# Warm-up matmuls in groups behind landings, last blocks loaded in parts, last deviation by a matmul, and step 1's output added by GpSimd

## What is computed

```python
def _gn(v, G=32, eps=1e-05):
    g = v.reshape(B_, G, C_ // G, H_, W_)
    m = jnp.mean(g, axis=(2, 3, 4), keepdims=True)
    s = jnp.var(g, axis=(2, 3, 4), keepdims=True)
    return ((g - m) / jnp.sqrt(s + eps)).reshape(v.shape)
def step(prev, x_i):
    y = jnp.einsum('oc,nch->noh', Wc, prev) + conv_b[None, :, None]
    y = jnp.where(y >= 0, y, prelu_a * y)
    cur = y + x_i
    return (cur, cur)
x = jnp.moveaxis(feature, 3, 0)
_, fwd_rest = jax.lax.scan(step, x[0], x[1:])
fl = jnp.concatenate([x[0:1], fwd_rest], axis=0)
_, bwd_rest = jax.lax.scan(step, fl[-1], fl[:-1], reverse=True)
out = jnp.concatenate([bwd_rest, fl[-1:]], axis=0)
...
x = x + _L0_conv_ref(_gn(x), L0_conv_conv_w, L0_conv_conv_b, L0_conv_prelu_a)
```

## Time and the profile before

| | us |
|---|---|
| median of 3 runs | 387.96 (387.77 to 388.16) |
| the profiled execution | 387.43 |
| its span | 385.7 |
| TensorE busy in it | 349.6 |
| VectorE busy in it | 288.8 |
| ScalarE busy in it | 225.6 |

### The profile page before, as it was taken

The page is one execution under the profiler, slowest core; times in us unless marked ns, Lnnn a source line. Parts: engine busy times, 40 slices in busy tenths (PEclk is TensorE's granted clock), DMA queues, the critical chain, the costliest instruction groups (busy, mean ns, idle before and its releaser), DMA issues.

```text
span 385.7 us, 10022 instructions
## 1 busy us (share of the span) xinstructions
PE 349.6 (91%) x3062; PEld 348.4 (90%) x3062; DVE 288.8 (75%) x945; ACT 225.6 (59%) x802; POOL 17.7 (5%) x24
## 2 busy tenths in 40 slices
PE   0116899999999999999999999999999999999993
PEld 0116899999999999999999999999999999999993
DVE  2886688888888878765565787787778778778774
ACT  3654265665665565566566566556656656655653
POOL 1177100000000000000000000000000000000000
PEclk9999899999999999999999999999999999999998
DMA  8997000000000000000000022112212212211222
GB/s 289 425 418 284 0 2 1 0 0 0 1 0 0 1 0 0 1 0 0 0 0 0 27 81 82 69 67 83 81 55 82 82 54 82 82 66 70 82 79 85
DMA packets 11242, 26.31 MB, mean 68 GB/s; under 512 B 1377, under 2 KB 2273, under 8 KB 11233
## 3 DMA queue, kind: packets, MB, share of 16 engines
q1 hardware_dynamic: 11088, 26.22, 17.7%
q10 hardware_dynamic: 144, 0.00, 0.0%
HBM read 13.63 MB, written 12.58 MB: 68 GB/s over the span
## 4 chain that ended last, share of the span: by engine, by line
PE 89%; DMA 6%; SPq 3%; DVE 1%; issue 1%; ACT 0%; DVEq 0%
PE psum L236 86%; DMA xin<-in_x 6%; SPq L171 3%; PE psum L218 1%; PE psum L208 1%; ACT above L273 0%; DVE state L373 0%; PE psum L197 0%; DVEq L47 0%; DVE state L368 0%; PE psum L190 0%; DVE bstat L285 0%; DVE chan L299 0%; ACT below L275 0%; PE psum L192 0%
## 5 line engine op out<-in xcount | busy, mean ns | idle before, releaser
L236 PE MATMUL psum<-state,w_t 128*128 (+1 forms) x2976 | 332.8, 275 | 0.2 <-DVE state L373 0.2
L236 PEld LDWEIGHTS psum<-state,w_t 128*128 128x128 f32 x2976 | 332.5, 192 | 0.5 <-DVE state L373 0.3
L273 ACT ACTIVATE above<-psum,params 128x128 f32<-128x128 f32 x376 | 139.7, 372 | 139.3 <-PE psum L236 129.0
L368 DVE TENSOR_TENSOR state<-above,state 128x128 f32 (+1 forms) x376 | 108.3, 288 | 70.0 <-ACT above L273 62.5
L275 ACT ACTIVATE below<-psum,negative 128x128 f32<-128x128 f32 x376 | 140.0, 372 | 0.0
L373 DVE SCALAR_TENSOR_TENSOR state<-below,negative,state 128x128 f32 (+1 forms) x376 | 123.4, 349 | 7.0 <-DVE state L368 0.4
L408 DVE TENSOR_TENSOR state<-state,xin (+1 forms) x48 | 32.9, 684 | 0.0
L285 DVE BATCH_NORM_STATS2 bstat<-xin 128x6 f32<-128x512 f32 (+2 forms) x38 | 23.1, 649 | 10.0 <-DMA xin<-in_x 9.9
L320 DVE TENSOR_SCALAR state<-xin,mean,rstd 128x320 f32<-128x320 f32 (+2 forms) x69 | 27.2, 437 | 0.2 <-POOL rstd L434 0.2
L190 PE MATMUL psum<-chan,same_group 128*128 128x4 f32 (+2 forms) x10 | 2.4, 310 | 27.1 <-DVE chan L299 27.1
L190 PEld LDWEIGHTS psum<-chan,same_group 128*128 128x128 f32 x10 | 2.1, 262 | 27.4 <-issue 15.1
(11 more groups left out here) (20 smaller groups left out, 19.9 us busy)
## 6 DMA issues: line engine op xcount, KB each, us to landing
out_y<-state SPq DMA_DIRECT2D x47, 256.0 KB, 2.0
xin<-in_x SPq DMA_DIRECT2D x14, 768.0 KB, 14.8
xin<-in_x SPq DMA_DIRECT2D x5, 256.0 KB, 3.5
w_t<-in_w SPq DMA_DIRECT2D x4, 256.0 KB, 11.6
out_y<-state SPq DMA_DIRECT2D x4, 64.0 KB, 1.7
xin<-in_x SPq DMA_DIRECT2D x1, 128.0 KB, 16.9
xin<-in_x SPq DMA_DIRECT2D x2, 64.0 KB, 14.8
params<-in_par ACTq DMA_DIRECT2D x1, 2.5 KB, 3.0
```

The costliest lines, as they stand in the source:

```text
L236: mm = nc.tensor.matmul(psum[:, 4 * par + o, 0:COLS], w_t[:, k, o * P:(o + 1) * P], xs[k], start=k == 0, stop=k == 3)
L273: nc.scalar.activation(above[:, par, o, :], z, ACT.Relu, bias=params[:, o:o + 1], scale=1.0).then_inc(above_done, 1)
L368: nc.vector.tensor_tensor(sts[o], above[:, par, o, :], sts[o], ALU.add).then_inc(part_done, 1)
```

## The change

The twelve warm-up matmuls go. In their place stand six groups (`keep_up`), each behind a landing and each a loop with two matmuls in a turn: 8 matmuls behind block 10, 6 behind block 12, 4 behind the second part of block 13, 4 and 6 behind the two parts of block 14, and 4 behind the second part of block 15. Block 0 is loaded in one piece, and blocks 13 and 14 in two (16 and 32 columns). ScalarE reduces the first unit of blocks 13 and 15 and none of block 14. The deviations and variances of a batch are read by VectorE after the first and second unit of the next tile's first block. For the last batch, of one column, a matmul with `centre` (one on the diagonal less `same_group`) gives the deviation, and one VectorE operation squares it. Step 0's matmuls stand in another order, two of them ahead of the last batch. GpSimd's early products follow each its difference. Column 1 is added by GpSimd into `spare`, the place of column 47, once that column is stored. The tiles of column 0 are stored as three and one.

```diff
-FIRST_A = [(0, 0), (0, 1), (0, 2), (0, 3)]
-FIRST_B = [(1, 0), (1, 1), (1, 2), (1, 3), (2, 0), (2, 1), (3, 0), (3, 1), (2, 2), (3, 2), (2, 3), (3, 3)]
+FIRST = [[(0, 0), (0, 1)],
+         [(1, 0), (2, 0), (0, 2), (0, 3), (1, 1), (1, 2)],
+         [(3, 0), (2, 1), (3, 1), (2, 2), (3, 2), (1, 3), (2, 3), (3, 3)]]
...
-FIRST_PIECES = [16, 16, 16]
-LAST_PIECES = [16, 16, 8, 4, 4]
+PIECES = {13: [16, 32], 14: [16, 32], 15: [16, 16, 8, 4, 4]}
+
+BY_ACT = {**{b: 2 for b in (0, 1, 2, 4, 5, 6, 8, 9, 10, 12)}, 13: 0, 15: 0}
...
+KEEP_UP = {(10, 0): 4, (12, 0): 3, (13, 1): 2, (14, 0): 2, (14, 1): 3, (15, 1): 2}
...
-            for i in range(FWD):
+            for i in range(FWD - 1):
                 step = W - 1 - i
                 sp.wait_ge(out_ready, i + 1)
-                sp.dma_start(out[step], state[:, step, :, :]).then_inc(stored, 16)
-            for o in range(KT):
-                sp.wait_ge(state_ready, 4 * (STEPS - 1) + o + 1)
-                sp.dma_start(out[0, :, o, :], state[:, 0, o, :]).then_inc(stored, 16)
-            sp.wait_ge(stored, 16 * (FWD + KT))
+                sp.dma_start(out[step], state[:, step, :, :]).then_inc(early_stored if i == 0 else stored, 16)
+            sp.wait_ge(spare_ready, 1)
+            sp.dma_start(out[1], spare).then_inc(stored, 16)
+            sp.wait_ge(state_ready, 4 * (STEPS - 1) + KT - 1)
+            sp.dma_start(out[0, :, 0:KT - 1, :], state[:, 0, 0:KT - 1, :]).then_inc(stored, 16)
+            sp.wait_ge(state_ready, 4 * STEPS)
+            sp.dma_start(out[0, :, KT - 1, :], state[:, 0, KT - 1, :]).then_inc(stored, 16)
...
+                if n1 - n0 == 1:
+                    nc.tensor.matmul(gdev, centre[:, :], chan[:, k, n0:n1, 0], start=True, stop=True).then_inc(dev_done, 1)
...
+            def keep_up(b, i):
+                pe.wait_ge(x_loaded[b][i], 16)
+                with pe.Fori(0, KEEP_UP[b, i]):
+                    for _ in range(2):
+                        nc.tensor.matmul(idle, same_group[:, :], same_group[:, :], start=True, stop=True)
...
+                if n1 - n0 == 1:
+                    dve.wait_ge(dev_done, 1)
+                    nc.vector.tensor_scalar(dev2[:, k, n0:n1], gdev, gdev, None, ALU.mult).then_inc(dev2_done, 1)
+                    dve.wait_ge(gmean_done, t + 1)
...
-            loop(dve, FWD, STEPS, slot_out)
+            loop(dve, FWD, STEPS - 1, slot_out)
+            slot(False)(STEPS - 1, (STEPS - 1) % 2)
...
+            pool.wait_ge(early_stored, 16)
+            pool.wait_ge(state_ready, 4 * (STEPS - 1))
+            nc.gpsimd.tensor_tensor(spare.rearrange("p k (n h) -> p (k n) h", n=N), state_step(pool, 1),
+                                    xin_step(pool, 1), ALU.add).then_inc(spare_ready, 1)
```

More of the change, by code:

```diff
@@ L145, in units @@
         def units(b):
[L147 to L153, removed]
+            found = []
+            begin = 0
+            for i, size in enumerate(pieces(b)):
+                for w0 in range(begin, begin + size, UNIT):
+                    found.append((w0, min(w0 + UNIT, begin + size), i))
+                begin += size
+            return [(w0, w1, i, BY_ACT.get(b) == nth) for nth, (w0, w1, i) in enumerate(found)]
         def record(b, i):
@@ L162, in scan_program @@
         act_blocks = [b for b in range(NBLK) if any(u[3] for u in units(b))]
+        spare = state[:, W - 1, :, :]
         block = ctx.enter_context(nc.Block())
@@ L213, in _ @@
             pe.wait_ge(group_made, 1)
-            for t in range(len(BATCHES) - 1):
-                if t == len(BATCHES) - 2:
-                    pe.wait_ge(x_loaded[NBLK - 2][0], 16)
-                    for _ in range(WARM_UP):
-                        nc.tensor.matmul(psum[:, 5, 0:P], same_group[:, :], same_group[:, :], start=True, stop=True)
+            pe.wait_ge(centre_made, 1)
+            for t in range(2):
                 group_means(t)
                 group_variances(t)
-            last = len(BATCHES) - 1
-            group_means(last)
-            first_units(FIRST_A)
-            group_variances(last)
-            first_units(FIRST_B)
+            keep_up(10, 0)
+            group_means(2)
+            group_variances(2)
+            keep_up(12, 0)
+            keep_up(13, 1)
+            keep_up(14, 0)
+            keep_up(14, 1)
+            keep_up(15, 1)
+            group_means(3)
+            group_variances(3)
+            first_units(FIRST[0])
+            group_means(4)
+            group_variances(4)
+            first_units(FIRST[1])
+            first_units(FIRST[2])
             def slot(forward):
@@ L286, in unit_stats, with block_stats @@
                                           x_part(b, w0, w1))
-            def block_stats(b):
-                for i, (_, _, _, by_act) in enumerate(units(b)):
-                    if not by_act:
+            def block_stats(b, between=()):
+                between = list(between)
+                for i, u in enumerate(units(b)):
+                    if not u[3]:
                         last = unit_stats(b, i)
+                        if between:
+                            between.pop(0)()
                 last.then_inc(stats_done, 1)
@@ L315, in variances @@
                 dve.wait_ge(gvar_done, t + 1)
[L316 to L317 removed]
+                nc.vector.tensor_scalar(var_eps[:, k, n0:n1], gvar(t), EPS, None, ALU.add).then_inc(var_done, 1)
             def normalise(n, k, w0, w1):
@@ L328, in _ @@
             for b in range(NBLK - 1):
-                block_stats(b)
+                t = b // N - 1
+                block_stats(b, (lambda: deviations(t), lambda: variances(t)) if t >= 0 and b % N == 0 else ())
                 if b % N != 0:
@@ L351, in _ @@
             dve.wait_ge(rstd_done, 4)
-            normalise(0, 3, 0, EARLY)
-            variances(4)
-            normalise(1, 3, 0, EARLY)
-            normalise(2, 3, 0, EARLY)
+            for n in range(N - 1):
+                normalise(n, KT - 1, 0, EARLY)
+                if n == 0:
+                    variances(4)
             dve.wait_ge(mean_kept, 5)
@@ L430, in _ @@
                                     channel_multiplier=-1).then_inc(group_made, 1)
+            pool.wait_ge(group_made, 1)
+            nc.gpsimd.tensor_scalar(centre[:, :], same_group[:, :], -1.0, None, ALU.mult).then_inc(centre_step, 1)
+            pool.wait_ge(centre_step, 1)
+            nc.gpsimd.affine_select(out=centre[:, :], in_=centre[:, :], compare_op=ALU.not_equal,
+                                    fill=1.0 - 1.0 / GROUP, base=0, pattern=[[-1, P]],
+                                    channel_multiplier=1).then_inc(centre_made, 1)
             pool.wait_ge(counts_set, 2)
```

64 lines of the change are left out of this document (33 added, 31 removed).

## The result

The changed kernel took 381.87 us (median of 4 runs, 380.97 to 382.78), the kernel before 387.87 beside it: a ratio of 0.9849, 95% interval 0.9813 to 0.9885. So the change is worth 4.8 to 6.0 us; 4.45 was forecast, and both medians lie in the range given. Two things are not as in the prediction: the terms that make up the sum, and how far apart the runs of this one kernel lie, 379.68 to 383.11 in ten.

The account below looks back on a forecast made before the run. TensorE's recurrence was taken to bound the kernel, leaving only time before step 1 and after the last step: 387.43 - 2.4 - 0 - 2.05 = 383.0, plus 0.53 for the runs' median, 383.5 us; range 381.3 to 385.3.

Parts of the forecast that it names:

- three things that were to show it wrong: Clock falling before step 1, groups ending well before or after 38.7, or step 1's store still under way at the last tile.
- The end, 2.4: After the last step: GpSimd adds column 1 early, so the last store issues at 381.15 instead of 383.51; gain 2.4 us.
- 0.5 us of cover: At the end: if GpSimd slows VectorE's addition for step 2, that has 0.5 us to spare before the next tile.
- The loads, 0 (at most 0.2): Loads of x: same bytes in 22 loads, and VectorE's long idle time ended on TensorE; 0, at most 0.2 us either way.
- The groups, 0 (from +1.8 to -0.3): Warm-up groups before step 0: end at 38.7 as before, gain 0; +1.8 for an end at 36.9, -0.3 at 39.0.
- full clock through the groups: Rival, warm-up: matmuls behind block 10 keep TensorE at full clock, groups end at 36.9; 6.25 us less, 381.7; chance 0.22.
- The order after the last statistic: Last statistic to step 1: step 1 at +4.3 instead of +6.35 us, gaining 2.05; with low clock about +5.7, gaining 0.6.
- The rule that I weighed against the row: Trainium skill's rule: clock falls come from long idle gaps between matmul bursts; by it no fall would come before step 1.
- the sparse stretch: From 38.7 to 40.7, before the first step: TensorE busy 0.74 of 2.00 us, after which the granted clock fell.

Follow-up runs that it names:

- the run with thirds: The changed kernel with block 0 loaded in three parts again instead of whole: 383.99 us, ratio 0.9915.
- The second trace: Profiled execution, 383.11 us, of the changed kernel run again with no edit; that series has a median of 382.77 us.

## Why the prediction was right

The number was right, and most of the working behind it was not. Two of the three things that were to show it wrong came about: the clock fell before step 1 in both traces of the changed kernel, and the groups ended at 35.16 and 37.29, well before 38.7. The forecast of 383.5 rested on 2.4 + 0 + 2.05. Point by point:

- **The end, 2.4: right in its mechanism, 0.2 to 0.5 too large.** It was 2.2 in the trace and 1.9 alone. GpSimd took 1.58 us where the nearest row had 1.04, which was hidden, and it slowed VectorE beside it, which was not quite: 0.2 on the path. I had given it 0.5 us of cover for the addition of step 2; the operation it met was the next one.
- **The loads, 0 (at most 0.2): wrong.** This is the first of two steps that failed. I argued that the same number of loads and bytes, and an idle time that ends on TensorE, leave nothing. But the warm-up matmuls were themselves behind block 14's landing, so a landing moved the idle time's end, and the whole load of block 0 moved every landing. Alone it gave 1.6 us. I knew of that wait and did not price an earlier landing. In the changed kernel the last landing came 1.1 to 1.2 us earlier than before; block 0's load accounts for 0.2 to 0.4 of that by the run with thirds, and where the rest comes from is not shown.
- **The groups, 0 (from +1.8 to -0.3): right for the common execution, and missed as a distribution.** The forecast's 38.7 was a start at 31.5 and 7.2 us of work. The second trace has 7.29 us of work from 30.00 on, the first 5.60 from 29.55 on. The earlier starts come with the earlier landings. Whether the rise comes in the groups or ahead of them decides their length, and it does not come at a fixed place. I had "full clock through the groups" as a rival with 0.22, for all executions; it is a case of single executions.
- **The order after the last statistic: the two values, 4.3 at the full clock and 5.7 with a fall, came out as 4.48 and 5.83.** The single instants fit too: behind the last statistic the squared deviation was done at 0.69 us (0.7 forecast) and GpSimd's power at 2.08 (2.1). But I took the full clock for the likelier, and that is the second step that failed. In both traces of the changed kernel the clock fell. The 2.05 was 0.5 there. The rule that I weighed against the row, that only long idle gaps bring a fall, does not tell this case: the clock fell at 37.80 with TensorE busy for 2.96 of the 3.40 us ahead of it. Nor does the sparse stretch bring the fall each time: where the rise came late, at 35.77 without the matmuls behind block 10 and at 38.70 with the old warm-up, the clock held through the same stretch.

So the sum of the common execution, read from the second trace, is 1.2 (landings) + 0.4 (groups and the statistics' order) + 0.5 (order after the last statistic) + 2.2 (end), less 0.1 for the longer last step: 38.95 is 1.68 earlier than before, of which 1.24 are the last landing. That is 4.3 in the spans (385.7 to 381.4), rounded terms apart. It comes out near the forecast's 4.45 by luck: the landings gave 1.2 us that were put at nothing, and the order gave 1.5 us less than forecast.

## What to carry to other kernels

A term that is costed at nothing because another wait covers it has to be traced to what starts the cover: here the covering matmuls waited for the landing in question. Where warm-up work is meant to bring the clock up, look at several executions, not one profile, and place it so that it does so in the worst of them; fourteen matmuls more, with two of step 0 moved, narrowed the spread from 3.4 to 1.4 us. And if the clock rises, check that it holds through the sparse stretch before the dense work: two warm-up matmuls, and two of step 0 moved ahead of the last batch, kept 1.1 us here.

## What was not expected of the hardware

- The shape of the first load moved all the later landings. In the windows from 0 to 28 us both kernels moved nearly the same: 376 GB/s, 10.53 MB, before, 382 and 10.70 MB with block 0 whole. At 420 GB/s the difference of 0.17 MB is 0.4 us. Yet block 12 was complete 1.54 us earlier (28.16 against 29.70). The delay is there in full from block 1 on: it landed at 9.00 against 7.44, and then both kernels land a block every 1.9 us. When block 12 landed, the transfers had moved 11.2 MB in the kernel before and 10.7 with block 0 whole, so more of the blocks behind it was already there. That the parts of a load are spread further over time would explain it, but no run shows why they would be. In the changed kernel with thirds, block 1 landed at 8.04 against 7.42, and the same edit cost only 0.6 us of landing there. What sets the delay is open.

```profile
0.00:28.00 28.00, 3.18 (x12) 2.86 (x12) 17.66 (x45) 15.12 (x37) 8.42 (x15) 1.00 0.94 376
```

```profile
0.00:28.00 28.00, 3.17 (x12) 2.85 (x12) 19.11 (x47) 15.13 (x37) 9.98 (x16) 1.00 0.94 382
```

The first of these rows is of the kernel before, the second of it with block 0 whole.

- GpSimd's two-input operation of 512 elements took 1.58 us with two full tensors, and 1.04 where one input was a broadcast of a few numbers. The broadcast need not be the reason: the long one began at 373.23, beside a VectorE addition of two full tensors that ran until 373.68, and 0.45 of the 0.54 us more could be a wait for that one. Every run had this overlap, so the two are not separated.
- A VectorE operation with two inputs in SBUF that began beside a two-input GpSimd operation ended just behind that one, in both places where the traces show it: 0.81 us for three elements a partition instead of 0.16, and 0.74 for 128 elements instead of 0.29. One with an input in PSUM kept its 0.16 us.
